# A transformer layer with a delta-rule scan: the products of the scan's outputs all on GpSimd, VectorE's second sum behind the second residual

## What is computed

```python
def step(S, inp):                       # one token; S is (batch, head, 8 values, 8 keys)
    kt, qt, vt, bt = inp
    err = jnp.einsum('bhvk,bhk->bhv', S, kt) - vt
    S = S - bt[..., None, None] * err[..., None] * kt[..., None, :]
    o = jnp.einsum('bhvk,bhk->bhv', S, qt)
    return (S, o)
S, o = jax.lax.scan(step, S0, (km, qm, vm, bm))
...
o = _rms(o, out_norm_w) @ Wout.T
x = x + o
h2 = _rms(x, mlp_norm_w)
x = x + silu(h2 @ Wgate.T) * (h2 @ Wup.T) @ Wdown.T
```

## Time and profile before

| | |
|---|---|
| median of 3 runs | 1543.97 us (1537.77 to 1548.41) |
| the profiled execution, its own time | 1549.48 us |
| its span, first to last instruction | 1547.7 us |
| PE busy | 1138.0 us (74%) |
| DVE busy | 969.1 us (63%) |
| ACT busy | 477.7 us (31%) |
| POOL busy | 172.7 us (11%) |
| mean granted PE clock | 0.819 of 2.4 GHz |

### The profile page before, as it was taken

How to read it: one execution, slowest core, us unless ns; L and a number is a source line. 1 busy time by engine, 2 the same in 40 slices (tenths; PEclk the granted TensorE clock), 3 DMA queues, 4 the chain that set the end, 5 groups by cost and what they waited for, 6 DMA issues and landing times.

```text
span 1547.7 us, 22181 instructions
## 1 busy us (share of the span) xinstructions
PE 1138.0 (74%) x8568; PEld 752.1 (49%) x8568; DVE 969.1 (63%) x2520; ACT 477.7 (31%) x995; POOL 172.7 (11%) x251
## 2 busy tenths in 40 slices
PE   5378547878877777878877887878887887777037
PEld 3146414555546544665445553655445554565025
DVE  3421376866777576865677575865777576846941
ACT  1024402434323412443332422433333422342011
POOL 2000000400031000400030010400030000400300
PEclk8579757979879887899878887989878887999559
DMA  9430413042211413041211414051301403001000
GB/s 294 40 33 5 55 62 33 2 61 67 31 18 36 50 56 33 2 70 56 35 14 40 54 47 33 1 69 58 40 9 41 64 30 33 1 14 61 0 14 7
DMA packets 112426, 64.76 MB, mean 42 GB/s; under 512 B 49184, under 2 KB 106688, under 8 KB 112320
## 3 DMA queue, kind: packets, MB, share of 16 engines
q1 hardware_dynamic: 109264, 58.19, 22.2%
q10 hardware_dynamic: 3056, 5.15, 1.2%
HBM read 45.73 MB, written 17.17 MB: 41 GB/s over the span
## 4 chain that ended last, share of the span: by engine, by line
PE 45%; DVE 25%; DMA 9%; SPq 7%; ACT 7%; issue 7%; POOL 1%; DVEq 0%; POOLq 0%; ACTq 0%
PE bank L1415 8%; PE bank L1395 5%; PE bank L1400 4%; DMA k_stack<-k_pieces 4%; PE bank L1334 4%; DVE k_l L1112 3%; PE bank L1553 3%; PE bank L1504 3%; DVE lane_buf L327 3%; PE bank L1326 2%; PE bank L1372 2%; PE bank L1576 2%; DVE lane_buf L1082 2%; DMA q_stack<-m_rows 2%; DVE conv L973 2%
## 5 line engine op out<-in xcount | busy, mean ns | idle before, releaser
L649 ACT ACTIVATE probs<-bank 128x512 f32<-128x512 f32 x256 | 149.2, 599 | 164.5 <-PE bank L1400 164.2
L903 DVE TENSOR_REDUCE mx<-bank 128x2 f32<-128x320 f32 x256 | 123.4, 491 | 84.1 <-PE bank L1372 75.2
L1415 PE MATMUL bank<-probs,v_ext 128*16 128x128 f32 x2048 | 160.8, 283 | 15.7 <-ACT probs L649 14.7
L1367 PE MATMUL bank<-edge_mask,identb 128*128 128x64 bf16 x512 | 70.0, 227 | 100.8 <-DMA k_stack<-k_pieces 43.3
L327 POOL TENSOR_TENSOR lane_buf<-state,q_l 128x128 f32<-128x128 f32 x128 | 87.8, 715 | 486.6 <-DVEq L1107 486.6
L1395 PE MATMUL bank<-tri_mask,identb 128*128 128x512 bf16 x256 | 112.8, 441 | 30.2 <-DMA q_stack<-m_rows 30.2
L1082 DVE TENSOR_TENSOR lane_buf<-state,til 128x128 f32<-128x128 f32 x256 | 104.1, 407 | 19.4 <-POOL lane_buf L537 10.1
L1367 PEld LDWEIGHTS bank<-edge_mask,identb 128*128 128x128 bf16 x512 | 35.2, 109 | 160.3 <-DVE mx L903 71.4
L1400 PE MATMUL bank<-q_stack,k_stack 128*128 128x128 bf16 x1024 | 112.4, 239 | 0.0
L1415 PEld LDWEIGHTS bank<-probs,v_ext 128*16 128x16 f32 x2048 | 87.0, 98 | 49.5 <-ACT probs L649 26.1
L1400 PEld LDWEIGHTS bank<-q_stack,k_stack 128*128 128x128 bf16 x1024 | 89.3, 108 | 39.7 <-issue 16.3
(11 more groups left out here) (156 smaller groups left out, 1918.7 us busy)
## 6 DMA issues: line engine op xcount, KB each, us to landing
k_stack<-k_pieces SPq DMA_DIRECT2D x192, 64.0 KB
q_stack<-q_pieces SPq DMA_DIRECT2D x192, 32.0 KB
q_l<-lane_q SPq DMA_DIRECT2D x8, 512.0 KB, 4.0
k_l<-lane_k SPq DMA_DIRECT2D x8, 512.0 KB, 4.7
q_pieces<-conv SPq DMA_DIRECT2D x24, 128.0 KB, 2.1
k_pieces<-conv SPq DMA_DIRECT2D x48, 64.0 KB, 2.0
x<-in_x SPq DMA_DIRECT2D x8, 256.0 KB, 2.8
x_in<-in_x SPq DMA_DIRECT2D x8, 256.0 KB, 8.5
```

What stands on the lines that cost most here:

```text
L649: act.activation(probs[:, u % 3], score_bank[u % 3][:], ACT.Exp, scale=float(DK) ** -0.5).then_inc(exp_done, 1)
L903: dve.tensor_reduce(mx[:, g, 2 * v:2 * v + 2], bank[1 + u % 2][:, 0:2 * SPAN].rearrange("p (h k) -> p h k", h=2), AX.X, ALU.max).then_inc( ...
L1367: pe.matmul(edges[:, :, e * W:e * W + SUB], identb[:], edge_mask[:, e * SUB:(e + 1) * SUB].rearrange("p (o s) -> p o s", o=1) .broadcast_t ...
L1415: last = pe.matmul(bank[5][row:row + VE, col:col + W], v_ext[:, b, kb, h, :], probs[:, u % 3, (hp * 2 + kb) * W:(hp * 2 + kb + 1) * W], st ...
```

## The change

POOL gets `second_terms`: after DVE has summed the first half (new semaphore `reduced`), it makes the second half's products too, ahead of `ffn_bias` in its stream. In `terms_of` the four products of 128 elements become one of 512 (all four v at once, the query broadcast over v), so that a half is 8 instructions instead of 20. DVE keeps the two sums. The first stays where it was; the second moves from before `rests_second` to behind `second_residual`, just ahead of `output_norm`. The wait on `pairs_kept` goes.

```diff
--- before.py
+++ after.py
@@ -253,6 +253,7 @@
         held = sem("held")
         scanned = sem("scanned")
         terms_ready = sem("terms_ready")
+        reduced = sem("reduced")
         o_ready = sem("o_ready")
         o_out = sem("o_out")
         o_in = sem("o_in")
@@ -323,8 +324,8 @@
             qc = q_l[:].rearrange("p k (c i) -> p i c k", i=C)
             n_c = cs.stop - cs.start
             for i in steps:
-                for v in range(VR):
-                    engine.tensor_tensor(out_terms[:, v, :, i, 0:DK], state[:, cs, v, :, C], qc[:, i, cs, :], ALU.mult)
+                engine.tensor_tensor(out_terms[:, :, :, i, 0:DK], state[:, cs, :, :, C].rearrange("p c v k -> p v c k"),
+                                     qc[:, i:i + 1, cs, :].broadcast_to([128, VR, n_c, DK]), ALU.mult)
                 last = engine.tensor_tensor(
                     out_terms[:, :, :, i, DK:DK + C],
                     mm_[:, i, :, cs].rearrange("p j (o c) -> p o c j", o=1).broadcast_to([128, VR, n_c, C]),
@@ -502,6 +503,11 @@
                 pool.wait_ge(scanned, n + 1)
                 terms_of(pool, slice(0, NC_ // 2)).then_inc(terms_ready, 1)
 
+            def second_terms(n):
+
+                pool.wait_ge(reduced, n + 1)
+                terms_of(pool, slice(NC_ // 2, NC_)).then_inc(terms_ready, 1)
+
             def ffn_bias(n):
 
                 pool.wait_ge(x1_ready, n + 1)
@@ -542,6 +548,7 @@
                 steps = 0
                 if scan:
                     first_terms(t)
+                    second_terms(t)
                 if following:
                     ffn_bias(t + 1)
                 if scan:
@@ -1111,12 +1118,14 @@
                 cs = slice(half * NC_ // 2, (half + 1) * NC_ // 2)
                 return dve.tensor_reduce(o_l[:, :, cs], out_terms, AX.X, ALU.add)
 
-            def half_outputs(n):
-
-                dve.wait_ge(terms_ready, n + 1)
-                dve.wait_ge(pairs_kept, n + 1)
-                done(reduce_terms(0))
-                done(terms_of(dve, slice(NC_ // 2, NC_)))
+            def first_outputs(n):
+
+                dve.wait_ge(terms_ready, n * 2 + 1)
+                reduce_terms(0).then_inc(reduced, 1)
+
+            def second_outputs(n):
+
+                dve.wait_ge(terms_ready, n * 2 + 2)
                 reduce_terms(1).then_inc(o_ready, 1)
 
 
@@ -1194,11 +1203,13 @@
                 if front:
                     rests_first(t + 2)
                 if has_scan:
-                    half_outputs(t)
+                    first_outputs(t)
                 if front:
                     rests_second(t + 2)
                 if following:
                     second_residual(n, has_scan)
+                if has_scan:
+                    second_outputs(t)
                 if has_scan:
                     output_norm(t)
                 if following:
```

## The result

The change makes the kernel slower: 1646.72 us (median of 4 runs, 1645.17 to 1650.55) against 1541.83 us (4 runs), a ratio of 1.068, 95% interval 1.0635 to 1.0724. On another chip it was 1.065 (1.057 to 1.073). The forecast was 75 us more than before, 1619 us, range 1603 to 1641.

The account below looks back on a forecast made before the run. Bound: at `output_norm` the outputs' round trip arrives 1.4 us after PE's feed-forward net. Second sum's place 63.2, last body 2.5 and PE's clock 9.3 make 75.0 us on the median 1544.0: 1619 us, range 1603 to 1641.

Parts of the forecast that it names:

- What is late next: Second half's products, bodies 0 to 6: the 6.95 us freed on DVE falls before its wait for PE; gain 0.
- The second sum's place: Second sum behind the second residual: outputs ready 9.66 us later in body 2, 63.2 us over seven bodies.
- PE's clock: PE idle for 11 us before `output_sums`, so slower clock to `tok_c`'s transposes in six bodies: 9.3 us, bounds 0 and 14.
- The products of the first half: POOL's first half, 20 instructions to 8: ends 12 us before DVE wants it, so hidden, 0 us.
- POOL's wide product: One 512-element product on POOL: 1.6 us, bounds 1.30 and 2.83, so the second half costs 10.1 us.
- Rival A: POOL's 512-element product takes 2.83 us, like the four it replaces; second residual waits for POOL: 1642 us; chance 0.14.
- Rival B: Part of the shift is absorbed by a wait in the next attention; half of it gives 1581 us; chance 0.08.
- Rival C: At `output_norm` the outputs' path has slack and the net alone sets the body: about 11 us gained, 1533 us; chance 0.04.

Follow-up runs that it names:

- experiment 3: Kernel before with only the second sum moved behind the second residual, products left on DVE: 1617.87 us against 1546.86, ratio 1.047.
- Experiment 1: Kernel before with only POOL's first-half products in the wide form, 512 elements an operation: 1565.01 us against 1546.86, ratio 1.013.
- experiment 4: Kernel after with the first half's products back in the narrow form: 1622.84 us against 1546.86 for the kernel before, ratio 1.049.
- experiment 7: Kernel before with only DVE's second-half products in the wide form, POOL's narrow: 1537.83 us against 1546.86, ratio 0.9938.

## Why the prediction went as it did

- **"What is late next", right.** The freed DVE time fell in front of L953 (9.96 us idle), and none of it came back.
- **The second sum's place, right.** 63.2 us plus 0.94 of clock in six bodies against 67.4 measured, and 66.8 for this edit alone in experiment 3. The range's low end has a slip that decides nothing: the text names 6 us of scatter and subtracts 7.
- **PE's clock, 9.3 us, right in its sign and mis-sized.** Six of the bodies' L1534 did go from 1.13 to 2.1 us, 5.7 in all. But from there to the transposes of `tok_c` the seven bodies have 131.5 us before and 136.5 after: 5.0 more, nothing beyond L1534 itself. Body 0, whose 20.15 us I expected everywhere, went down to 18.67 although its L1534 took 2.07 both times. The 2.1 us more from the output norm to the next first product are no proof either: with the norm just as late, experiments 3 and 4 have 841.2 and 847.4 there, against 847.5 before.
- **The products of the first half, "hidden: 0", wrong.** This step failed, and with it the range. I asked only whether POOL would be done in time, which it was. I did not ask what POOL's instruction does to the engine beside it. Experiment 1 puts 18 us on it, experiment 4 about 25 (+76 against +101). Before the change, the same holds were there in small: the scan product took up to 849 ns, 384 as a rule. The line in the kernel before (ns smallest/median/largest) was there to be read:

```profile
L1082 DVE TENSOR_TENSOR lane_buf<-state,til x256: 368/384/849, 216.0 to 1469.7; 128x128 f32<-128x128 f32 x128
```

- **POOL's wide product, 1.6 us, mis-sized.** Measured 2.09 to 2.15, and 2.55 when DVE's L904 held it in turn. The second half took 12.35 us on POOL instead of 10.1, and 11.4 in the last body, where no L904 is beside it; there that made E 4.6 us longer instead of 3.2. The interpolation took the surcharge of the strided read as fixed per instruction; 0.71 us for 128, 1.15 for 256 and 2.09 for 512 show that it grows with the elements. The 1.1 us that the prediction worked out for a plain sum lay further off; L516, such a sum, took 1.30.
- **Rival A, wrong in its size, right in its place.** With 2.1 us POOL's bias ends 0.1 to 1.0 us ahead of the second residual in bodies 0 to 5, 3.2 in body 6. In body 0 it was even the last: PE's product ends at 323.49, POOL's bias at 323.67, DVE starts at 323.76. The profile names PE as the releaser all the same, so the name alone would have hidden it:

```profile
316.32 7.17 PE L1337 MATMUL bank<-w_dn,hid 128*128 128x256 f32 x32 [0.56 <-ACT hid L698]
```
```profile
322.26 1.41 POOL L516 TENSOR_TENSOR x_in<-x_in,b_dn 128x256 f32<-128x256 f32 x2
```
```profile
323.76 0.69 DVE L953 TENSOR_TENSOR x<-bank,x_in 128x512 f32<-128x512 f32 x1 [9.91 <-PE bank L1337]
```

- **Rival B, absorption, wrong**: stretch C arrives in the time almost whole. **Rival C, wrong for the change**, but the gap that it priced at 11 us is there, and experiment 7 collects some 6 of it (C 7.4 less, B 1.2 more).

In all: 75 forecast, 98 in the profiled executions. Of the 23 between them 22.4 are A and D. The rest nearly cancels: B and E gave 3.6 and 2.1 us more than forecast, C 1.4 less, PE's clock outside C 1.6 less, and the start and end of the program, which the change does not reach, 1.9 less. That the sum misses by just A and D is in part luck.

## What to carry to other kernels

Before you move work off a busy engine, find out what the chain waits for behind it: here a sum of 3.35 us started a round trip of 7.7 us over four engines, and putting it behind a wait cost three times its own length in each body. And work on an idle GpSimd is not free: a long GpSimd instruction held up each VectorE product with two SBUF inputs until it ended, so beside a chain of short VectorE products many short GpSimd operations beat few long ones, even though GpSimd itself is then busy for longer.

## What I had not expected of the hardware

- A DVE product of 128 elements with two SBUF inputs ends about 0.16 us after the POOL instruction that it met, be that one 0.9 or 2.1 us long, and the longer L904 (512 elements) 0.55 us after; sums with one input are untouched. It works in the other direction too: beside DVE's L904, POOL's L327 took 2.55 us instead of 2.09 and its L329 1.30 instead of 0.85.
- On DVE, a product of 512 elements takes 0.68 us with both inputs contiguous and 1.06 to 1.09 us when one or both of them jump from element to element.
- Fewer, longer instructions shorten GpSimd's own time (14.2 to 11.8 us a half) and lengthen the kernel's (by 1.3%).
